# Graph attention on one core: the gathered rows are added into the logit sums by accumulating transposes instead of fp32 products with the identity

## The reference

```python
x_l = (x @ W_l).reshape(n, H, C)
x_r = (x @ W_r).reshape(n, H, C)
e = (ea @ W_e).reshape(-1, H, C)
m = jax.nn.leaky_relu(x_l[src] + x_r[dst] + e, NEG_SLOPE)
alpha = jnp.einsum('ehc,hc->eh', m, att)
amax = jax.ops.segment_max(alpha, dst, num_segments=n)
expa = jnp.exp(alpha - amax[dst])
denom = jax.ops.segment_sum(expa, dst, num_segments=n)
a = expa / (denom[dst] + 1e-16)
out = jax.ops.segment_sum(x_l[src] * a[:, :, None], dst, num_segments=n)
```

## Time and profile before

| | |
|---|---|
| Median of 3 runs | 2239.63 us (2237.43 to 2239.76) |
| Span of the profiled execution, first to last instruction | 2234.5 us |
| Between median and span | 5.1 us |
| Own device time of the profiled execution | not listed apart from its span |
| PE, PEld, DVE, ACT, POOL busy | 1911.7, 1332.3, 1236.5, 1080.3, 871.6 us |
| Attention block, from the first gather's issue to the last join | 985.4 to 2129.9 us |
| Mean granted TensorE clock | 0.879 |

### The profile page before, as it was taken

One profiled execution on the slowest core, in us unless ns is written; L12 is line 12 of the kernel. 1 busy time (PEld: TensorE's weight loads), 2 busy tenths in 40 slices (PEclk: granted clock), 3 DMA queues, 4 the chain that ended last, 5 costly groups with the idle time before them and its releaser, 6 DMA issues. The chain is left out here.

```text
span 2234.5 us, 37102 instructions
## 1 busy us (share of the span) xinstructions
PE 1911.7 (86%) x11265; PEld 1332.3 (60%) x11265; DVE 1236.5 (55%) x2729; ACT 1080.3 (48%) x2477; POOL 871.6 (39%) x884
## 2 busy tenths in 40 slices
PE   4566666899889999967899999999999999898866
PEld 2455555655578887734466666666666666665544
DVE  4766666577744242466545545545555545555575
ACT  0355565677355333431345455545555545546435
POOL 1000000000000000037777777777777777777300
PEclk9555555699999999978999999999999999999877
DMA  2100000000124100033333333333333333333111
GB/s 71 61 1 1 1 1 1 8 0 0 29 75 128 41 1 6 1 88 89 93 94 97 87 95 96 88 99 94 88 98 93 89 94 94 86 100 89 43 34 29
DMA packets 132412, 133.33 MB, mean 60 GB/s; under 512 B 28969, under 2 KB 102274, under 8 KB 132226
## 3 DMA queue, kind: packets, MB, share of 16 engines
q1 hardware_dynamic: 104450, 73.76, 11.4%
q0 software_dynamic: 27776, 57.20, 10.3%
HBM read 126.05 MB, written 4.82 MB: 59 GB/s over the span
## 5 line engine op out<-in xcount | busy, mean ns | idle before, releaser
L2156 POOL DMA_INDIRECT rows<-x_l,src x856 | 848.2, 991 | 278.7 <-issue 253.3
L2353 DVE TENSOR_TENSOR bent<-psum,bent 128x512 f32<-128x512 f32 x214 | 147.7, 690 | 315.3 <-ACT bent L2280 315.0
L2280 ACT ACTIVATE bent<-psum 128x512 f32<-128x512 f32 x214 | 126.4, 591 | 398.5 <-PE psum L2183 376.2
L2240 PEld LDWEIGHTS psum<-both,node_hot 128*128 128x128 f32 x1712 | 233.4, 200 | 108.0 <-issue 102.1
L2183 PE MATMUL psum<-ident,rows 128*128 128x128 f32 x1712 | 245.8, 289 | 40.4 <-DMA rows<-x_l,src 39.0
L2240 PE MATMUL psum<-both,node_hot 128*128 128x144 f32 x1712 | 271.9, 307 | 2.8 <-DVE acc L2444 2.1
L770 ACT ACTIVATE counts<-psum (+1 forms) x181 | 181.3, 1002 | 176.3 <-PE psum L763 112.2
L2183 PEld LDWEIGHTS psum<-ident,rows 128*128 128x128 f32 x1712 | 218.9, 199 | 75.2 <-DMA rows<-x_l,src 66.0
L2307 ACT ACTIVATE apart<-iota,rel 128x128 bf16<-128x128 f32 x828 | 262.3, 388 | 0.1
L2177 PE MATMUL psum<-edges,w_e 32*128 32x512 f32 x428 | 242.1, 645 | 0.0
L1146 POOL TENSOR_TENSOR ht<-ht,mix_rows 128x512 f32<-128x512 f32 (+1 forms) x7 | 7.8, 1149 | 588.1 <-ACT mix_rows L1187 588.1
(11 more groups left out here) (343 smaller groups left out, 2405.9 us busy)
## 6 DMA issues: line engine op xcount, KB each, us to landing
rel_row<-e_rel_rows SPq DMA_DIRECT2D x107, 256.0 KB, 3.5
edges<-edge_t SPq DMA_DIRECT2D x428, 32.0 KB
rows<-x_l,src POOLq DMA_INDIRECT x856
edge_part<-edge_t SPq DMA_DIRECT2D x40, 320.0 KB, 3.1
ht<-x SPq DMA_DIRECT2D x6, 256.0 KB, 2.8
new<-e_new_before SPq DMA_DIRECT2D x12, 128.0 KB
new<-e_new_behind SPq DMA_DIRECT2D x12, 128.0 KB
x_l<-rows SPq DMA_DIRECT2D x4, 320.0 KB
```

What stands on the lines that cost most here:

```text
L2156: e.indirect_dma_start(rows[:, g % ring, j * ROW:(j + 1) * ROW], None, k.xl, bass.IndirectOffsetOnAxis(ap=src[:, at:at + 1], axis=0)).then ...
L2240: final = e.matmul(to, near_hot[:, at, j, :], both[:, at, j, :], start=j % 2 == 0, stop=j % 2 == 1)
L2353: e.tensor_tensor(bent[:, g % 3, :], z_banks[g % 3], bent[:, g % 3, :], ALU.max).then_inc(*leaky.up())
```

## The change

`join` passes one more argument to its four matmuls, `is_transpose=True`. Operands, order, waits and signals stay as they are; the four results are still added to what `begin` left in the bank (`start=False`).

```diff
--- before.py
+++ after.py
@@ -2181,7 +2181,7 @@
                     e.wait_ge(got[g % slots].sem, got[g % slots].at(4 * lap(g)))
                     for j in range(4):
                         final = e.matmul(z[:, j * P:(j + 1) * P], rows_at(g)[:, j * P:(j + 1) * P], k.ident[:, :],
-                                         start=False, stop=j == 3)
+                                         start=False, stop=j == 3, is_transpose=True)
                     final.then_inc(*joined.up())
```

## The result

The changed kernel takes 2246.02 us (median of 11 runs, 2236.39 to 2253.45) where the kernel before takes 2239.07 on the same chip (11 runs, 2231.94 to 2244.92). The ratio is 1.0035, with a 95% interval of 1.0019 to 1.0052: slower by 0.35%, where 0.42% faster was forecast. The profiled execution is its fastest, 2236.39 us with a span of 2234.6, as long as that of before (2234.5). The trace so shows where a gain went, and only a part of the loss.

A forecast was written before the change was run, and what follows sets the result against it. GpSimd's gather issues were taken to bound slots up to 182, TensorE mainly the last 31 of 214. Savings of 3.6 + 5.9 = 9.5 us gave span 2225.0, time 2230.1 us (0.42% faster), own range 2227 to 2233, 8-in-10 range 2226 to 2236.

The forecast's parts named there:

- Slots 0 to 182: nothing: The 183 early joins save some 83 us of TensorE's time, all beside GpSimd's issues, so no gain.
- the gathers keep their times: Slots 183 to 197: gathers unmoved, so join 197 starts no earlier than 2009.9, capping the gain before it at 3.1 us.
- GpSimd's row of issues itself changes its pace: Sign that the prediction is wrong altogether; gathers were expected within a few us of 985 to 2094.
- The saving in a join: Each join goes from 8 to 4 pairs: 0.45 us saved after sums, 0.50 us after L2177.
- rival 2: Joins: an accumulating transpose costs what the product does, nothing saved, 2239.6 us; chance 0.08.
- The floor of 1.6 us: Shortest time from the end of a gather's issue to its join; at this distance GpSimd sets the pace.
- under 2010: Sign for slots 183 to 197: a join 197 later than 2010 would make the catch-up step wrong.
- The late part: Slots 199 to 213: twelve joins count, 11 x 0.45 + 0.92 us, 5.9 us saved.
- rival 4: Clock falls more often, slower sums behind one or two late stops; 2233 to 2237 us; chance 0.18.
- the catch-up: Slots 183 to 197: TensorE catches up with the gathers by join 197; 3.6 us gained there.
- Rival 5: Half clock for a full double slot after four late stops, 5.2 us each, 2250.7 us; chance 0.05.
- Rival 1: All slots: TensorE is the bound after all, 214 x 0.45 = 96 us saved, 2143 us; chance 0.02.

The follow-up runs named there:

- head_only_2: Kernel before with transposes only in the joins of groups 0 to 182, products from 183 on, `weigh` whole; 2245.36 us, ratio 1.0038.
- head_in_four: Kernel before with transposes only in the joins of groups 0 to 182 and `weigh` cut into four instructions; 2225.16 us, ratio 0.9946.
- one_part_2: Kernel before, no transposes, `begin` adding only one of three bf16 parts of `x_r`, 0.50 us less a slot; 2240.74 us, ratio 1.0020.
- before_in_four: Kernel before, products in every join, with `weigh` cut into four instructions; 2236.26 us, ratio 0.9989.
- tail_only_2: Kernel before with transposes only in the joins from group 183 on, `weigh` whole; 2233.19 us, ratio 0.9984.
- filled_2: Changed kernel, all joins transposes, with three bf16 zero products filling the saved time in each slot up to group 182; 2238.37 us, ratio 0.9995.
- after: The changed kernel: transposes in all joins, `weigh` whole, against the kernel before; 2246.02 us, ratio 1.0035.
- after_2: The changed kernel measured again, unchanged, against the kernel before; 2244.13 us, ratio 1.0024.
- tail_only: Transposes only from group 183 on, on the chip where the kernel before takes 2481.94 us; 2480.29 us, ratio 0.9989.

## Why the prediction was wrong, point by point

**The step that failed** is "Slots 0 to 182: nothing", with "the gathers keep their times": I took 0.99 + 0.30 us a gather for a constant, when it was 0.94 + 0.30 and 41.8 us of holding by VectorE, which depends on when TensorE lets VectorE go. The 83 us saved there do lie beside GpSimd, as said, but they moved `weigh` onto the starts of gathers, which are held for 52.1 us in all with the change, the early ones by `weigh` alone for 22.8 in place of 13.9. Shown: the early joins are the loss (`head_only_2`), splitting the one instruction turns it into a gain (`head_in_four`), and a shorter slot without transposes does the same to the gathers (`one_part_2`). The prediction named the sign to look for, that "GpSimd's row of issues itself changes its pace", and gave it no chance of its own.

**The saving in a join was right:** L2183 x856, and the double slot 5.16 us in place of 5.61; rival 2 is out. The Trainium skill's fourfold saving for fp32 (in "TensorE: Matmul & The Clock Gate", section "Terms") isn't what the rows show: 5.61 - 5.16 is 0.45 us, a half. **The floor of 1.6 us was right:** join 197 (2017.17) is 1.9 us behind the end of its gather. It isn't under 2010 because that gather ends at 2015.3 in place of 2008.3, and 2010 hung on that.

**The late part was right but for one slot.** From join 199 to join 213 it is 96.58 us in place of 99.08, 2.5 less where 5.9 was said. Slot 208 alone grew from 12.92 to 15.86; the others shrank by 5.44. Timeline of that slot after its stop:

```profile
2091.99 1.94 PE L2194 MATMUL psum<-bent,att_heads 128*48 128x512 f32 x2 [4.59 <-DVE bent L2353]
2093.86 1.46 PE L2174 MATMUL psum<-hot,x_r_parts 128*128 128x256 bf16 x6
2095.25 2.07 PE L2177 MATMUL psum<-edges,w_e 32*128 32x512 f32 x2
...
2098.15 3.67 PE L2240 MATMUL psum<-both,node_hot 128*128 128x144 f32 x16
2101.66 0.60 PE L2183 MATMUL psum<-ident,rows 128*128 128x128 f32 x4
```

The stop is the one of the earlier trace rows and no longer by more than half a us, but the sums take 3.67 us where full clock gives 2.23: TensorE is at 1.2 GHz up to them and through most of them (granted clock 0.50 from 2092.0 to 2098.2, 0.58 from there to 2101.7). In the kernel before, the same sums were at full clock:

```profile
2096.04 2.23 PE L2240 MATMUL psum<-both,node_hot 128*128 128x144 f32 x16
```

That is rival 4's mechanism, at one stop and for 2.9 us. Slot 208 is 15.8 to 16.4 us in every trace with late transposes, but also 16.36 in `before_in_four`, without any, and 13.1 in `head_in_four`, with the same split and early ones; so transposes are not its only cause, and what sets its length stayed open. In `tail_only_2` the arithmetic closes: 9.5 forecast, less 2.9 for this slot, less 0.6 for held gathers of groups 183 to 198, is 6.0 us; its last join is 4.4 us earlier than before although its group 183 began 1.3 later, together 5.7.

**In the profiled execution** the account is: the gathers of groups 197 and 198 are 7.0 us later; the catch-up takes it down to 4.2 at join 197; 1.0 is won to join 199 and 2.5 to join 213, which leaves 0.7. So the late saving was real and paid for the early loss.

**Rivals 4 and 5** as a cause of the slower median: the clock is lower over the whole (0.856 in place of 0.879), but that lies mostly beside the gathers, and it doesn't rule the spread. Among the 12 runs of `head_only_2` the fastest, 2232.53 us, had clock 0.860, and the slower ones a higher one (correlation +0.59; +0.30 and +0.09 in the two sets of the changed kernel). Rival 5's 5.2 us a stop is not there. The Trainium skill's sentence that the full clock doesn't engage for transposes ("TensorE: Matmul & The Clock Gate", section "Part 4: PE-mode transpose") gets no support from the stretches above: `one_part_2`, with the shorter slot and none of its joins turned, has the same lower clock,

```profile
985.00:1101.00 116.00, 93.16 (x284) 49.05 (x284) 68.75 (x107) 12.63 (x24) 88.69 (x85) 0.71 0.35 90
1101.00:1927.00 826.00, 734.92 (x3629) 464.01 (x3629) 430.91 (x961) 424.85 (x1185) 632.75 (x635) 0.96 0.35 92
```

and `filled_2`, with every join turned and the time filled, has 0.85 and 0.97 there. The lower clock goes with the shorter slot. **Rival 1** was right to the extent that the early joins are worth something once the gathers are free of the weighing: 9.6 us, not 83.

**What stays open.** In `after`, `after_2` and `head_only_2` (early transposes, whole weighing) the profiled execution was the fastest of 11 or 12, 9 to 13 us under the median. Holding is seen there (52.1, 54.0 and 46.0 us in all, in place of 41.8), but what the slower executions add wasn't seen in any trace; that it is more holding is argued from the split, which gives 22 to 25 us back. Each kernel has one trace, and the same early code was held for 34.2 us in one and 40.5 in another. And no rule was found that tells from the phase in advance how much is held.

## What to carry to other kernels

A row of instructions that sets the pace isn't a constant: before counting on it, split its mean into the duration of the undisturbed ones and the rest, and look at what runs on the neighbouring engine when the long ones start. If something off the path moves that neighbour in time, the pace may change, up or down. Where GpSimd issues indirect transfers without a break, keep VectorE's instructions with two SBUF inputs short. (To read one input from PSUM is a guess from the rows of `bend` and `add`; no run tried it.) Here cutting one into four costs VectorE 0.2 us each time, makes the change worth having, and gives 2221.37 us, faster than either kernel; the later start on top (2218.66 us) is within the intervals of that. On the chip where GpSimd waits for the others, the early transposes brought 31 us without it.

## What the runs showed of the hardware

- A gather that starts while VectorE runs a two-input SBUF instruction is held until about 0.12 us before that one's end (0.40 us left at 1207.64, 0.28 held). One that goes ahead is not disturbed by a `weigh` behind it (0.94 us at 1204.65, with `weigh` from 1204.66); one that is held when `weigh` begins can be held on to that one's end (1.65 us at 1587.33, with `weigh` from 1587.48).
- A VectorE instruction that reads one tile and a column can hold a gather too: `one_hots` (`tensor_scalar`, int16 to bf16) with 0.24 us left makes the one of 1127.34 take 1.06 us. `bend` and `add`, which read PSUM and SBUF, hold none: 79 and 86 starts, 0.2 and 0.1 us in all.
- Four transposes that add to what the bank holds take as long as four plain ones, half of fp32 products: 0.44 us from start to start in a join behind sums in place of 0.89 (a double slot 5.16 us in place of 5.61).
- With a shorter TensorE slot the granted clock of the middle stretch is 0.95 (by transposes, `after`) or 0.96 (without, `one_part_2`) in place of 0.99, and of the first 0.72 or 0.71 in place of 0.84; with transposes and the time filled (`filled_2`) it is 0.97 and 0.85.
- Two chips differ by 243 us on the same kernel (2239 and 2482). The difference lies between the first gather and the last join: 1392 us in `tail_only` on the one (980.58 to 2372.96), 1144 in `tail_only_2` on the other (980.4 to 2124.5, traces of the same kernel).
